# Tile 0's second layer and the turning of its weights put behind tile 1's units, in a DLRM cross-interaction kernel on one core

## The reference

```python
e = jnp.stack([tbl_f[ids[:, f]] for f in range(32)], axis=1)      # 1024 x 32 x 32
x, res = e, []
for W in (W0, W1):                                                # 1024 x 128, 4096 x 128
    z = jnp.einsum('bhd,bmd->bhmd', e, x).reshape(b, -1, 32)
    x = jnp.einsum('bpd,pj->bjd', z, W)
    res.append(x)
z = jnp.sum(jnp.concatenate(res, axis=1), axis=-1)                # 1024 x 256
h = jnp.maximum(jnp.concatenate([z, dense_ctx], axis=1) @ W_top1 + b_top1, 0.0)
h = jnp.maximum(h @ W_top2 + b_top2, 0.0)
y = h @ W_top3
```

## Time and profile before

| what | value |
|---|---|
| time, median of 3 runs | 376.89 us (376.88 to 377.1) |
| span of the profiled execution | 597.7 us |
| PE busy in it | 412.6 us |
| POOL busy in it, 256 gathers | 246.5 us |
| ACT, DVE busy in it | 235.5, 203.4 us |
| mean granted clock of PE in it | 0.800 of 2.4 GHz |

### The profile page before, as it was taken

The page is one execution under the profiler, slowest core; times in us unless marked ns, Lnnn a source line. Parts: engine busy times, 40 slices in busy tenths (PEclk is TensorE's granted clock), DMA queues, the critical chain, the costliest instruction groups (busy, mean ns, idle before and its releaser), DMA issues.

```text
span 597.7 us, 9512 instructions
## 1 busy us (share of the span) xinstructions
PE 412.6 (69%) x3656; PEld 360.8 (60%) x3656; DVE 203.4 (34%) x834; ACT 235.5 (39%) x774; POOL 246.5 (41%) x262
## 2 busy tenths in 40 slices
PE   5512112874257887877788778687787679999988
PEld 4301001653256776766666667577676668989988
DVE  4200000694723333322333233333332235556510
ACT  3300000662175334522343334433452237676641
POOL 6777772547055444544445554544444440000000
PEclk9755555795589877877787888977787779999999
DMA  8100000000000000000000000000000000000000
GB/s 299 45 14 13 13 13 6 11 3 14 2 10 10 8 10 7 10 8 9 9 9 10 10 10 9 11 8 9 8 10 8 8 10 2 2 2 2 2 2 1
DMA packets 10765, 9.66 MB, mean 16 GB/s; under 512 B 4664, under 2 KB 8896, under 8 KB 10720
## 3 DMA queue, kind: packets, MB, share of 16 engines
q0 software_dynamic: 8192, 4.21, 4.8%
q1 hardware_dynamic: 2528, 4.84, 2.3%
HBM read 9.03 MB, written 0.00 MB: 15 GB/s over the span
## 4 chain that ended last, share of the span: by engine, by line
PE 57%; issue 18%; another core or an unknown queue 11%; DVE 7%; ACT 6%; DMA 1%; SPq 0%; ACTq 0%
PE WA L725 20%; PE QB L697 10%; PE PA L687 8%; PE T L710 4%; DVE RT L421 4%; PE M L738 4%; PE M L757 2%; PE ET L674 2%; ACT eblk L285 2%; ACT TS L285 1%; PE PA L639 1%; PE M L764 1%; PE M L748 1%; ACT RT L285 1%
## 5 line engine op out<-in xcount | busy, mean ns | idle before, releaser
L278 POOL DMA_INDIRECT emb<-in_table,rows x256 | 245.8, 960 | 239.0 <-PE ET L674 165.3
L725 PE MATMUL WA<-TS,RX 128*128 128x128 f32 x896 | 127.0, 301 | 1.0 <-ACT TS L285 1.0
L584 DVE COPY TS<-T 32x64 f32<-32x64 f32 x256 | 55.5, 217 | 200.6 <-PE T L710 184.6
L725 PEld LDWEIGHTS WA<-TS,RX 128*128 128x128 f32 x896 | 119.7, 215 | 6.0 <-issue 6.0
L697 PE MATMUL QB<-eblk,zQ 128*64 128x68 f32 x1024 | 69.1, 243 | 74.3 <-issue 74.0
L697 PEld LDWEIGHTS QB<-eblk,zQ 128*64 128x64 f32 x1024 | 49.9, 146 | 89.8 <-issue 85.8
L552 DVE TENSOR_TENSOR zQ<-ET,eT 128x1024 f32<-128x1024 f32 x32 | 39.2, 1225 | 159.0 <-ACT eT L285 158.9
L687 PE MATMUL PA<-eblk,zP 128*128 128x132 f32 x512 | 80.6, 296 | 5.3 <-issue 3.4
L639 PE MATMUL PA<-sym,TS 128*128 128x272 f32 x64 | 29.4, 552 | 74.5 <-issue 47.3
L687 PEld LDWEIGHTS PA<-eblk,zP 128*128 128x128 f32 x512 | 73.4, 212 | 6.3 <-issue 4.9
L285 ACT ACTIVATE eblk<-ET 32x256 f32<-32x256 f32 x128 | 48.6, 380 | 71.0 <-PE ET L674 66.0
(11 more groups left out here) (87 smaller groups left out, 294.1 us busy)
## 6 DMA issues: line engine op xcount, KB each, us to landing
emb<-in_table,rows POOLq DMA_INDIRECT x256
TS<-in_W SPq DMA_DIRECT2D x8, 256.0 KB, 4.3
wt<-in_W_top SPq DMA_DIRECT2D x2, 512.0 KB
y1w<-in_W_rows SPq DMA_DIRECT2D x1, 448.0 KB
TS<-in_W_rows SPq DMA_DIRECT2D x1, 448.0 KB
sym<-in_W_cols SPq DMA_DIRECT2D x1, 264.0 KB, 2.8
TS<-in_W_cols SPq DMA_DIRECT2D x1, 264.0 KB, 3.1
idc<-in_ids SPq DMA_DIRECT2D x1, 128.0 KB, 2.0
```

The source lines that it names most:

```text
L278: eng.indirect_dma_start(emb[par][:, g, :], None, table, bass.IndirectOffsetOnAxis(rows[:, k, g:g + 1], 0))\
L584: eng.tensor_copy(view(ts[32 * q:32 * q + 32, :, :], P * REST + b0, [[4 * P, 2], [P, 4], [1, 8]]), view(src, q, [[C17, 2], [4, 4], [C33, 8 ...
L725: m = eng.matmul(WA[:, 0:P], C[:, kt, :], TS[k % 2][:, slot_of(kt), :], start=(kt == 0), stop=(kt == KT - 1))
```

## The change

The second layer of tile 0 is no longer spread over tile 1's slots. The weights are turned in tile 1's last three slots (21 to 23) instead of tile 0's last four, and all 56 matmuls of tile 0's second layer and its 7 of the first follow in slot 23; its tower stands in slots 25 to 27, in tile 2, beside tile 1's. All other tiles stay as they were. ACT's copies are put in the order that this needs: the last unit's copies of tile 1 stand ahead of the last banks of `C`. DVE's late sums are cut into six pieces and stand ahead of a unit's products instead of behind them; `own_sums(0)` stands between the products of unit 0 and unit 1. The transposes of units 0 and 1 stand behind steps 12 and 22 instead of 8 and 18. The loads of `base` and `raw` go through ACT's queue, at its start.

```diff
--- before.py
+++ after.py
@@ -212,9 +212,10 @@
 
 
         Y2_PER = 7
-        C_AT = SLOTS_TILE - 4
-        C_TO = (0, 3, 6, 10, CB)
+        C_AT = 2 * SLOTS_TILE - 3
+        C_TO = (0, 3, 7, CB)
         Y1_AT, L1_AT, L2_AT, Y_AT = 8, 9, 10, 11
+        FIRST_L1, FIRST_L2, FIRST_Y = 2 * SLOTS_TILE + 1, 2 * SLOTS_TILE + 2, 2 * SLOTS_TILE + 3
 
 
         L1_BANKS = (PA[0][:, 0:P], PA[1][:, 0:P], QB[0][:, 0:P], QB[1][:, 0:P])
@@ -223,28 +224,30 @@
         def y2_range(t):
 
             k, j = divmod(t, SLOTS_TILE)
-            if k > 0 and j < KT // Y2_PER:
+            if t == 2 * SLOTS_TILE - 1:
+                return 0, range(KT)
+            if k > 1 and j < KT // Y2_PER:
                 return k - 1, range(Y2_PER * j, Y2_PER * j + Y2_PER)
             return None
 
         def tile_at(t, step):
 
             k, j = divmod(t, SLOTS_TILE)
-            if k >= 1 and j == step:
+            if t == {Y1_AT: 2 * SLOTS_TILE - 1, L1_AT: FIRST_L1, L2_AT: FIRST_L2, Y_AT: FIRST_Y}[step]:
+                return 0
+            if k > 1 and j == step:
                 return k - 1
             return None
 
 
-        EARLY_AT = (8, 18)
+        EARLY_AT = (12, 22)
 
         block = ctx.enter_context(nc.Block())
 
         @block.sync
         def _(eng):
             eng.dma_start(idc[:, :, :], ids).then_inc(ids_loaded, 16)
-            eng.dma_start(base[:, :], bases).then_inc(ids_loaded, 16)
             eng.dma_start(sym[:, :], w0_cols[0]).then_inc(w0_loaded, 16)
-            eng.dma_start(raw, w0_cols[1]).then_inc(w0_loaded, 16)
             per = F // W1P
             for i in range(W1P):
                 eng.dma_start(w1s[:, per * i:per * i + per, :], w1[:, per * i:per * i + per, :]).then_inc(w1_loaded[i], 16)
@@ -369,6 +372,8 @@
                 copy(y[k % 2][:, :], M[0:1, 0, :]).then_inc(y_kept, 1)
 
 
+            eng.dma_start(base[:, :], bases).then_inc(ids_loaded, 16)
+            eng.dma_start(raw, w0_cols[1]).then_inc(w0_loaded, 16)
             eng.wait_ge(const_s, 2)
             copy(h2[:, 0, 0:1], ident[:, 0:1]).then_inc(table_loaded, 1)
             eng.wait_ge(table_loaded, 1)
@@ -385,11 +390,15 @@
                 if r == 0 and len(EARLY_AT) <= u + 1 < ALL:
                     eblk_copy(u + 1)
                 part_copy(t)
-                if r == 0 and u > 0:
+                if r == 0 and u > 0 and u != 2 * UNITS:
                     across_copy(u - 1)
-                if r < 2 and u > 0:
+                if r < 2 and u > 0 and u != 2 * UNITS:
                     rest_copies(u - 1, r + 2)
-                if C_AT <= t < SLOTS_TILE:
+                if t == 2 * SLOTS_TILE - 1:
+                    across_copy(u)
+                    for j in range(2, NQ):
+                        rest_copies(u, j)
+                if C_AT <= t < 2 * SLOTS_TILE:
                     for q in range(C_TO[t - C_AT], C_TO[t - C_AT + 1]):
                         c_copy(q)
                 pieces = y2_range(t)
@@ -505,28 +514,38 @@
                 cross_first(0, 0, SUB, early_first)
                 apart_across(1, 0, 0, HALF, False, early_first)
                 cross_first(1, 0, HALF, late_first)
+
+            def early_sums_second():
                 eng.wait_ge(early_first, 2 * SUB + 1)
                 both_across(0, 0, SUB, True, added)
                 cross_second(0, 0, SUB, added)
                 apart_across(1, 0, 0, HALF, True, added)
 
             def late_sums(part):
+
                 if part == 0:
                     eng.wait_ge(rt_kept, F)
                     eng.wait_ge(rx_kept, F // 2)
                     both_across(0, SUB, SUB, False, late_first)
+                if part == 1:
                     cross_first(0, SUB, SUB, late_first)
                     apart_across(1, 1, 0, HALF, False, late_first)
+                if part == 2:
                     for X in range(2):
                         rest_across(X)
                         rest_own(X)
                         rest_same(X)
-                if part == 1:
-                    own_sums(1)
-                if part == 2:
+                    for e in range(2):
+                        own_adds(1, e, False)
+                if part == 3:
+                    eng.wait_ge(own_first[1], 2 * SUB)
+                    for e in range(2):
+                        own_adds(1, e, True)
+                if part == 4:
                     eng.wait_ge(late_first, 2 * SUB + 2)
                     both_across(0, SUB, SUB, True, added)
                     cross_second(0, SUB, SUB, added)
+                if part == 5:
                     apart_across(1, 1, 0, HALF, True, added)
                     cross_second(1, 0, HALF, added)
 
@@ -603,21 +622,23 @@
                         eng.memset(eblk[i][DIM * v:DIM * v + DIM, :, v, one], 1.0).then_inc(ones_set, 1)
             eng.wait_ge(y1_loaded, 16 * 2)
             eng.tensor_tensor(y1w[:, :, :], y1w[:, :, :], raw_y1, ALU.add).then_inc(y1w_made, 1)
-            for u in range(len(EARLY_AT)):
-                for part in range(3):
-                    products(u, part)
+            for part in range(3):
+                products(0, part)
             eng.wait_ge(rt_kept, HALF)
             own_sums(0)
+            for part in range(3):
+                products(1, part)
             early_sums()
+            early_sums_second()
             for u in range(ALL):
                 if u > 0:
                     for part in range(3):
                         rest_copies(u - 1, part)
+                if u < 6:
+                    late_sums(u)
                 if len(EARLY_AT) <= u + 1 < ALL:
                     for part in range(3):
                         products(u + 1, part)
-                if u < 3:
-                    late_sums(u)
             for part in range(3):
                 rest_copies(ALL - 1, part)
             eng.wait_ge(tower_loaded, 16 * 5)
```

## The result

The change takes **393.28 us** (median of 4 runs, 390.07 to 395.28) against 376.88 (4 runs, 376.8 to 377.1): 1.0424 times as long, 95% interval 1.039 to 1.0458, or 16.4 us more. The forecast was 384.7, the range ended at 392. The profiled execution has a span of 392.5 us and a time of 394.32; so 1.8 us lie around the span, not the 5.8 that the prediction left for it. In the comparisons of this document, single runs that took over 1.5% more than the fastest of their kernel are left out.

The account below looks back on a forecast made before the run. Before, PE's path (368.7 us) and the gathers' path (366.1 + L) were almost level; after, gathers end tile 1 and PE's dense work follows: 373.9 + L, with L = 5 378.9, plus 5.8 around the span, 384.7 us; range 374 to 392.

Parts of the forecast that it names:

- L: On POOL, the time that DVE's sums keep gathers waiting; put between 0 and 18.65 us, taken as 5.
- both sums: The rebuilt path ends: gathers' path before, 366.1 us plus L; path through tile 1's end after, 373.9 us plus L.
- the same instructions: DVE's sums in six pieces: instructions unchanged, products of units 2 to 4 between them; PE's 7.3 us wait goes.
- The rebuild from a starved profile: Kernel before, rebuilt from unstarved stretches: turning of the weights at 72.6 us, unit 8's start at 128.9 us.
- The gathers: On POOL: first at 4.16 us, 0.45 sooner after; pitch 1.25, landing 2.2; 41.0 us follow unit 31's transposes.
- What lies around the span: Time outside the span of the kernel before, left over once L was taken as 5: 5.8 us.
- DVE done at 91.6: DVE's sums, products up to unit 7 and rest copies end at 91.6 us, before unit 8's last gather lands.
- Second layer and turning: On PE behind tile 1: unit 7 and turning 20, second layer 12.8, first 1.6, tower 5.0; together 39.4 us.
- A: Rival, faster: DVE, not gathers, ends tile 1; -3.1 us, 373.8 us; chance 0.17.
- B: Rival, no change: gathers set the end in both kernels; the change gives 0.45 us, 376.4 us; chance 0.08.
- C: Rival, much slower: every RX sum holds gathers, 18.65 us, pitch at most 1.22; end 390.4 us, +13.5; chance 0.16.

Follow-up runs that it names:

- the tiny sums: Each sum cut to one column per operand, instructions, order and waits kept: the change so edited took 377.82 us, the kernel before so edited 368.25 us.

## Why the prediction was wrong

The direction and the mechanism were right: the landing of gathers says when tile 1 ends, and then PE has a dense stretch alone. The terms behind the landing came within 1 us. **The step that failed is that one L stands in both sums**, because the six pieces were taken as "the same instructions" and what they do to the gathers was put at nothing. L was 9.6 us in the kernel before and 17.6 in the change (15.1 in a second execution).

"I take L = 5" was wrong too, but didn't move the forecast by itself. What isn't L was put around the span, so with one L over 2.6 in both sums the forecast is 373.9 + L + (376.89 - 366.1 - L) = 384.7, whatever L is.

- *The rebuild from a starved profile.* Turning at 72.6, unit 8 at 128.9: measured 71.62 and 128.90. Right to 1 us; that unit 8 fits to the last digit is luck, as the turning came 1.0 us sooner and what follows took 1.0 longer.
- *The gathers.* First at 4.16 and 0.45 sooner: the first starts at 4.00 to 4.28 in the four profiles with the old start and at 3.97 to 4.17 in the ten with the new one, so no gain shows. Pitch 1.25, landing 2.2 against 2.3 to 2.4, 41 us behind unit 31: right. That gathers set the end of the kernel before followed only from L over 2.6; with 9.6 it is so, and the tiny sums show it by 9 us. The gather at 112.00 passed sums of RT with RT, but the third piece, such sums alone, held one (1.93 us).
- *What lies around the span.* 5.8 was what the choice of L left over. It is 1.8, and with it L in the kernel before follows: 376.89 - 1.8 - 366.1 = 9.0, against 9.6 measured. The prediction had the bound ("at most 8 to 11 us for L and for what lies around the span") and chose the middle of it.
- *Sums in six pieces: "the same instructions".* This is where the forecast went wrong. The instructions are the same and PE's wait for QC goes, but a gather that meets a short piece is mostly held to its end, and behind a first block there are now five such pieces in place of two. L is 17.6 in the profiled run (15.1 in another). Sum: 373.9 + 17.6 = 391.5 against a span of 392.5; before 366.1 + 9.6 = 375.7 against 375.8. At one L the two differ by the predicted 7.8, which the tiny sums measure as 8.7; the 8.0 by which L differs is the rest of the 16.7 us between the spans.
- *DVE done at 91.6.* The 91.9 at which the last piece ends is close by luck. The 91.6 stood for the sums and all products up to unit 7 without a gap; those of unit 7 run from 105.61 to 108.84, since DVE too waits for landings, by way of ACT's copies (4.81 us before 105.61). That DVE isn't what ends tile 1 was right: PE has no wait for it.
- *Second layer and turning.* 39.4 us of dense work were predicted (with 5.0 in tile 2); 35.0 + 4.8 came. Right. What makes it cost was seen only in part: PE waits for landings at the start of units 2 to 7 (25.7 us in all, 15.4 of them in tile 1), and, as the run with only the second layer late shows, to ACT's copies, 3.2 us a unit, which the second layer had covered.
- *Rivals.* A: landings, not DVE, ended tile 1; out. B: out, PE had no wait for a landing behind 112.88, so in the change gathers don't set the end. C had the nearest time (390.4), and for the change nearly the right L (18.65), but not its mechanism: it wanted every RX sum to hold, in both kernels, and a pitch of 1.22. The pitch is 1.25, and in the kernel before six gathers pass amid the first block.

That sums cause the holding is shown: with the tiny sums nearly nothing is held. The Trainium skill, SBUF — State Buffer, section "SBUF: two separate sides", says that of a VectorE instruction with two SBUF inputs and a GpSimd instruction that reads SBUF, the one that starts first has the port pair that the two engines share for its whole length, and the other is blocked. The rows at 36.33 and 48.97 agree that a gather is blocked, but by a whole row of sums, not by one: the first 25 of the block take 6.34 us, 0.25 each.

Where a gather can come through, the traces show in part. The sums with RX get shorter from 128x112 to 128x16 and start again. First a row of the kernel before profiled again, then one of the change:

```profile
41.55 0.18 DVE L421 TENSOR_TENSOR RT<-RT,RX 128x16 f32<-128x16 f32 x1
...
41.21 0.22 DVE L430 TENSOR_TENSOR RT<-RT,RX 128x16 f32<-128x16 f32 x1
```

In the first the shortest sum ends at 41.73, and the gather of 40.25 comes through at 42.34, 0.61 us behind it. All 38 gathers over 1.3 us that came through while sums with RX went on, in the eleven profiles with full sums, ended 0.60 to 0.74 us behind such an end. The first block has one every 1.4 to 2.4 us, a later piece one at most. But the gather of 36.33 let the end at 41.43 go by, which the second row shows, and three more. What lets one gather through there and not another stays open: the order of work ahead was tried both ways and doesn't settle it.

## What to carry to other kernels

Before splitting a block of VectorE work into pieces "at no cost", look at what else runs beside it: here each piece caught one gather, and most held it to their end, so many short pieces cost more than the same work in a few long blocks. Work moved out of another engine's waits has to be priced by what then fills those waits (nothing, here), not only by its own time. And when two kernels are compared by a sum, an unknown that stands in both should be asked twice: does the change alter it?

## What the hardware showed that was not expected

A gather takes 0.94 us of POOL, or some 2.1 amid a long block of sums, or anything up to the whole block (9.63 us). The same program gave 17.6 and 15.1 us of held time in two executions, with spans of 392.5 and 388.9; that may well be the spread of its runs (390.07 to 395.28), though only two of them were profiled. The first 25 sums of the block took 6.34 us both where a gather was held throughout and where gathers passed (and 6.34 in the earlier trace rows). The starved state of the earlier trace rows came in one execution and in none of the profiles of these runs.
